# A graph layer whose spilled node terms are written to the output early and completed there by accumulating DMAs

## The reference, cut to what matters

```python
h = jnp.maximum(_layernorm(x, axis=-1), 0.0)          # 100000 nodes x 64
z = jnp.concatenate([h[src], h[dst], edge_attr], -1)   # 25000 edges x 160
m = jax.nn.sigmoid(z @ W_f + b_f) * jax.nn.softplus(z @ W_s + b_s)
message = jax.ops.segment_sum(m, src, num_segments=100000)
mean = jnp.mean(message, axis=0)
var = jnp.mean((message - mean) ** 2, axis=0)
normed = (message - mean) * jax.lax.rsqrt(var + 1e-5) * gamma + beta
return x + h + normed
```

## Time and profile before

| | before |
|---|---|
| median of 3 runs | 1061.29 us (1059.76 to 1061.81) |
| the profiled execution: its own time | 1060.81 us |
| its span, first to last instruction | 1059.1 us |
| first stage, about | 0 to 846 us |
| scan | 846 to 924 us |
| variance, scale and shift | 924 to 927 us |
| final stage | 927 to 1059 us |
| busy share of the span: PE, DVE, ACT, POOL | 60%, 69%, 51%, 69% |
| bytes moved by DMA | 176.07 MB |

### The profile page before, as it was taken

How to read it: one execution, slowest core, us unless ns; L and a number is a source line. 1 busy time by engine, 2 the same in 40 slices (tenths; PEclk the granted TensorE clock), 3 DMA queues, 4 the chain that set the end, 5 groups by cost and what they waited for, 6 DMA issues and landing times.

```text
span 1059.1 us, 11028 instructions
## 1 busy us (share of the span) xinstructions
PE 631.5 (60%) x2458; PEld 453.8 (43%) x2458; DVE 733.2 (69%) x1547; ACT 540.0 (51%) x1181; POOL 729.9 (69%) x652
## 2 busy tenths in 40 slices
PE   0474665666566666656766666676556689944232
PEld 0252444454444444444544454554445578810000
DVE  3884675757575686766777666776666569699788
ACT  1263654545454665545565464655646564434322
POOL 6777878787877877777878777787878752430700
PEclk9855565555555565556555555655656689955555
DMA  8997534343434334333443333433433399799999
GB/s 320 397 394 275 126 96 106 96 106 94 106 94 106 74 86 87 61 81 61 79 87 61 80 71 70 87 63 79 85 56 59 35 380 420 247 302 426 413 404 377
DMA packets 88183, 176.07 MB, mean 166 GB/s; under 512 B 42575, under 2 KB 49299, under 8 KB 79699
## 3 DMA queue, kind: packets, MB, share of 16 engines
q1 hardware_dynamic: 35851, 115.32, 30.9%
q0 software_dynamic: 42880, 20.09, 15.4%
q10 hardware_dynamic: 9416, 40.29, 9.3%
HBM read 107.12 MB, written 68.53 MB: 166 GB/s over the span
## 4 chain that ended last, share of the span: by engine, by line
POOL 48%; DMA 24%; issue 17%; DVE 6%; PE 3%; ACT 1%; SPq 1%; POOLq 0%; ACTq 0%; DVEq 0%
POOL msgs_dram L607 24%; POOL m_buf L594 24%; DMA m_buf<-msgs_dram 8%; DMA msgs_dram<-y_kept 8%; DMA msgs_dram<-sums,target 6%; PE ps_all L1544 2%; DVE m_buf L1795 2%; DMA out_dram<-m_buf 2%; DVE m_buf L1801 1%; DVE sums L1717 1%; PE ps_all L1539 0%; SPq L499 0%; POOL m_buf L617 0%; DVE target L794 0%; DVE m_buf L763 0%
## 5 line engine op out<-in xcount | busy, mean ns | idle before, releaser
L594 POOL DMA_INDIRECT m_buf<-in_x_dram,m_buf x384 | 366.9, 955 | 118.7 <-issue 109.4
L607 POOL DMA_INDIRECT msgs_dram<-sums,target x184 | 289.7, 1574 | 56.2 <-issue 55.8
L1171 PE MATMUL ps_all<-sums,m_last 128*128 128x64 f32 x920 | 188.5, 394 | 124.8 <-ACT m_last L1033 107.1
L1171 PEld LDWEIGHTS ps_all<-sums,m_last 128*128 128x128 f32 x920 | 181.0, 303 | 136.2 <-issue 112.5
L719 DVE TENSOR_REDUCE m_last<-late 128x24 f32<-128x1536 f32 (+1 forms) x49 | 85.3, 1742 | 87.8 <-ACT late L984 87.8
L1131 PE MATMUL ps_all<-ident,m_buf 128*128 128x128 f32 x192 | 53.0, 431 | 128.6 <-DVE m_buf L809 128.6
L1145 PEld LDWEIGHTS ps_all<-m_buf 128*128 128x128 f32 x392 | 91.9, 322 | 49.0 <-issue 49.0
L794 DVE TENSOR_TENSOR target<-moved,m_last 128x4 int32<-128x4 f32 x49 | 9.6, 196 | 146.1 <-POOLq L605 145.8
L1033 ACT ACTIVATE m_last<-m_last,one_col 128x512 f32<-128x512 f32 x196 | 107.6, 550 | 1.6
L1131 PEld LDWEIGHTS ps_all<-ident,m_buf 128*128 128x128 f32 x192 | 34.9, 217 | 160.4 <-DVE m_buf L809 138.5
L1143 PE MATMUL ps_all<-m_buf 128*128 128x512 f32 x98 | 98.8, 1111 | 0.0
(11 more groups left out here) (171 smaller groups left out, 1078.1 us busy)
## 6 DMA issues: line engine op xcount, KB each, us to landing
m_buf<-msgs_dram SPq DMA_DIRECT2D x38, 1024.0 KB, 11.9
m_buf<-in_x_dram SPq DMA_DIRECT2D x48, 512.0 KB, 5.0
msgs_dram<-y_kept SPq DMA_DIRECT2D x14, 1536.0 KB, 11.0
out_dram<-m_buf ACTq DMA_DIRECT2D x20, 1024.0 KB, 11.2
m_buf<-src_rows_dram SPq DMA_DIRECT2D x47, 256.0 KB, 4.1
y_spill_dram<-y_kept ACTq DMA_DIRECT2D x19, 512.0 KB
y_kept<-y_spill_dram SPq DMA_DIRECT2D x8, 1024.0 KB, 12.1
m_buf<-in_x_dram,m_buf POOLq DMA_INDIRECT x392, 2.5
```

The costliest lines, as they stand in the source:

```text
L594: pool.indirect_dma_start(xg[:, n % G_SLOTS, 2 * j + c, :], None, x, bass.IndirectOffsetOnAxis(ap=ids[:, c, n * TILES + j:n * TILES + j + ...
L607: pool.indirect_dma_start(msgs, bass.IndirectOffsetOnAxis(ap=target[:, n % UNROLL, j:j + 1], axis=0), comb[:, n % COMB_SLOTS, j, :], None, ...
L1171: pe.matmul(ps_c[:, j, :], same_of(b, j, j + 1)[:, 0, :], msg_of(g)[:, b, :], start=(b == 0 and not begun), stop=(b == j), skip_group_chec ...
```

## The change

- ACT writes the spilled y straight to its rows of the output (`at.out_rows`), and nothing loads it again.
- The list `order` is now: the 8 held blocks, block 24, the spilled blocks 0 to 9 (i = 9 to 18), then blocks 10 to 15 (i = 19 to 24). For a spilled block DVE computes message * scale and adds shift from SBUF; POOL then issues an accumulating DMA of the block onto the output (`merge`). The loads that take over these buffers wait for its landing (`merged`). The three groups of four patches stand on POOL between merges.
- For the 15 other blocks ("kept parts") PE adds the whole shift as an fp32 product of one row. No part has its mean taken or beta added ahead, and `split_shift` is gone.
- Blocks 13 to 23 have 20 rows squared, where blocks 13 to 21 had 16 and blocks 22 and 23 had 12; the three banks are used from block 15 on, not 19.

```diff
-SQ_THEN_ROWS = 16
+SQ_THEN_ROWS = 20
-SQ_CHANGE = 19
+SQ_CHANGE = 15
...
-            act.dma_start(y_spill[:, bass.ds(row, BULK), :],
+            act.dma_start(at.out_rows[:, bass.ds(row, BULK), :],
                           y_kept[:, bass.ds(row, BULK), :]).then_inc(spilled, 16)
...
-        if b >= NB - 1 - FEW_SQUARED:
-            return [(0, n, FEW_ROWS)]
...
-    order = held + [NB - 1] + list(range(SPILLED_BLOCKS, NB - 1 - M_BUFS)) + list(range(SPILLED_BLOCKS))
+    order = held + [NB - 1] + list(range(SPILLED_BLOCKS)) + list(range(SPILLED_BLOCKS, NB - 1 - M_BUFS))
...
+    def wait_stored(eng, i):
+
+        eng.wait_ge(merged[buf_of(i)] if merges(i) else stored[buf_of(i)], 16 * stores_of(i))
...
         for k, i in enumerate(in_ring[M_BUFS:]):
             r0, n = BLOCKS[order[i]]
-            sp.wait_ge(stored[buf_of(i)], 16 * stores_of(in_ring[k]))
+            wait_stored(sp, in_ring[k])
             sp.dma_start(m_buf[:, buf_of(i), 0:n, :], m_rows[:, r0:r0 + n, :]).then_inc(m_loaded[buf_of(i)], 16)
-            for b in y_loads[Y_AHEAD + k:Y_AHEAD + k + 1]:
-                load_y(b)
...
             for c in range(0, n, BANK_ROWS):
                 w = min(BANK_ROWS, n - c)
-                ins = pe.matmul(ps_y(k)[:, c:c + w, :], weights, row.unsqueeze(1).to_broadcast([row.shape[0], w, F]),
+                ins = pe.matmul(ps_y(k)[:, c:c + w, :], ones[0:1, :],
+                                shift[0:1, :].unsqueeze(1).to_broadcast([1, w, F]),
                                 start=False, stop=True, skip_group_check=True)
...
-        for k in range(Y_FIRST, BETA_PARTS):
-            add_row(k, ones[0:1, :], bet[0:1, :])
-        pe.wait_ge(split_done, 1)
-        for k in range(BETA_PARTS, len(y_parts)):
-            add_row(k, ones_b[:, :], shift_row[0:SPLIT, :])
+        pe.wait_ge(shift_ready, 1)
+        for k in kept_parts:
+            add_row(k)
...
+        def merge(i):
+
+            k = next(k for k, (of, _, _) in enumerate(y_parts) if of == i)
+            r0, n = BLOCKS[order[i]]
+            pool.wait_ge(added, k + 1)
+            pool.dma_start(out_rows[:, r0:r0 + n, :], m_out(i, 0, n), accum_op=ALU.add).then_inc(merged[buf_of(i)], 16)
...
+            if merges(i):
+                dve.tensor_tensor(m, m, shift[:, :].unsqueeze(1).to_broadcast([P, n, F]), ALU.add).then_inc(added, 1)
+            else:
+                dve.wait_ge(y_summed, kept_parts.index(k) + 1)
+                dve.tensor_tensor(m, m, ps_y(k), ALU.add).then_inc(added, 1)
```

More of the change, by code:

```diff
@@ L1281, in stage_two @@
     stored = [sem(f"stored{i}") for i in range(M_BUFS + 1)]
+    merged = [sem(f"merged{i}") for i in range(M_BUFS)]
     rest_stored = sem("rest_stored")
@@ L1366, in wait_m, with merges @@
             eng.wait_ge(m_loaded[b], 16 * loads)
+    def merges(i):
+        return order[i] < SPILLED_BLOCKS
     def stores_of(i):
-        return len([k for k, _, _ in y_parts if k <= i and buf_of(k) == buf_of(i)])
+        return len([k for k, _, _ in y_parts if k <= i and buf_of(k) == buf_of(i) and merges(k) == merges(i)])
+    def wait_stored(eng, i):
+        eng.wait_ge(merged[buf_of(i)] if merges(i) else stored[buf_of(i)], 16 * stores_of(i))
     def y_of(b):
[L1374 to L1387, removed]
+        r0 = BLOCKS[b][0] - SPILL * BULK
+        return y_kept[:, r0:r0 + BLOCKS[b][1], :]
     def part_rows(i):
@@ L1393, in stage_two @@
                for r in range(0, BLOCKS[b][1], part_rows(i))]
[L1395 to L1398, removed]
+    kept_parts = [k for k, (i, _, _) in enumerate(y_parts) if not merges(i)]
+    bank_of, filled = {}, 0
+    for k in kept_parts:
+        bank_of[k] = filled % PSUM_BANKS
+        filled += (y_parts[k][2] + BANK_ROWS - 1) // BANK_ROWS
+        assert bank_of[k] * BANK_ROWS + y_parts[k][2] <= PSUM_BANKS * BANK_ROWS
     def banks(k):
@@ L1406, in held_by @@
     def held_by(k):
-        return max([j + 1 for j in range(k) if banks(j) & banks(k)], default=0)
+        return max([j + 1 for j in kept_parts if j < k and banks(j) & banks(k)], default=0)
     first_held = BLOCKS[held[0]][0]
@@ L1507, in scalar @@
         act.activation(var[:, :], lnv[:, :], ACT.Exp, scale=-0.5).then_inc(rstd_ready, 1)
-        copied = Y_FIRST + 1
+        waiting = kept_parts[Y_FIRST + 1:]
         for k in range(-1, len(y_parts)):
-            if k >= 0:
+            if k >= 0 and not merges(y_parts[k][0]):
                 i, r, n = y_parts[k]
@@ L1524, in scalar @@
         for k in range(M_BUFS + 1):
-            last = max(i for i in range(NB) if buf_of(i) == k)
+            last = max(i for i in range(NB) if buf_of(i) == k and not merges(i))
             act.wait_ge(stored[k], 16 * stores_of(last))
@@ L1799, in vector @@
             dve.wait_ge(scaled, k + 1)
-            dve.wait_ge(y_summed, k + 1)
-            dve.tensor_tensor(m, m, ps_y(k), ALU.add).then_inc(added, 1)
+            if merges(i):
[3 more added lines that the diff above has]
+                dve.tensor_tensor(m, m, ps_y(k), ALU.add).then_inc(added, 1)
             if i == len(held) - 1 and y_parts[k + 1][0] > i:
```

96 lines of the change are left out of this document (26 added, 70 removed).

## The result

The changed kernel takes 1091.47 us (median of 4 runs, 1091.09 to 1094.87), the kernel before 1061.15 (1059.76 to 1061.81, 4 runs). The ratio is 1.0295, with a 95% interval of 1.0271 to 1.0318: the change costs 30 us. The prediction said 1083 in a range of 1066 to 1109, slower with a chance of 88%.

A forecast was written before the change was run, and what follows sets the result against it. Bounds: PE in the scan, DMAs in the final stage. First merge at 990.0 after PE's slow row, then 82.7 us of DMAs, 7 of patches, about 1 of landing: span 1081; plus 1.7 and 0.5 gives 1083 us, range 1066 to 1109.

The forecast's parts named there:

- the scan's gain: Scan: shift ready about 4.8 us earlier, with bounds of nothing and 8 us.
- Shift is ready near 922.4: End of scan: DVE, no longer PE, sets the end; shift ready near 922.4, against 927.2 counted before.
- a scan that still ends at 923: Scan: listed sign that the forecast is wrong; if right, the diagonal starts near 919, after DVE.
- the bound that the prediction named: Scan: the gain of about 4.8 us becomes nothing if ACT and DVE stop each other over their three banks.
- PE's row at 1.2 GHz sets the pace for nine blocks: Final stage, first 9 blocks: PE's fp32 row takes 1.71 us a bank, 60.9 us in all, 922.4 to 983.3.
- DVE through the merged blocks, 43.1 us: Final stage, spilled blocks: DVE at its own pace, 9 x 4.52 + 2.4 = 43.1 us, from 985.5 to 1028.6.
- A merge costs 2 units: Final-stage DMAs: accumulating a block takes 2 units, a unit being 2.545 us of all engines for a full block.
- From the first added block to the end, 91 us: Final stage from 990.0 to 1081: 32.5 units or 82.7 us, 7 us of patches, about 1 us of last landing.
- Rival 3: Final stage: PE's clock rises to 2.4 GHz, first 9 blocks end 21 us earlier; chance 12%, of which 8 faster.
- 49.4 units: Final stage before the change: 15.5 units of second loads, 9.5 of spilled y, 24.4 of stores; 126 us.
- 17 + 32.5 = 49.5 units: Final-stage DMAs after the change: 17 units (43 us) in the first nine blocks, 32.5 (82.7 us) from the first merge.

The follow-up runs named there:

- e11: Changed kernel with the three groups of patches put behind merges 9, 11 and 13 instead of from the 14th on: 1090.72 us, ratio 1.0279.
- e3: Changed kernel with PE adding shift as an fp32 product of 128 equal rows (shift/128 each) instead of one row: 1075.37 us, ratio 1.0140.
- e10: Changed kernel with the 128-row product and 20 rows squared only in even blocks from 14 on, merges kept: 1070.93 us, ratio 1.0094.
- e9: Kernel before (y reloaded) without means, beta rows and split, with the 128-row product and 20 rows squared only in even blocks from 14: 1060.31 us, ratio 0.9998.
- e1_plain: Changed kernel whose ten merges store and do not add, so outputs of spilled rows lack y: 1074.88 us, ratio 1.0137.

## Why the prediction was right, and what it mis-sized

The direction and the mechanisms of the final stage held; the scan's gain did not come, and with it and the tail go the 8.4 us between the span forecast (1081) and measured (1089.4). By its own steps:

- **Shift is ready near 922.4: wrong, it was 928.5**, later than before (927.7 in the trace, 927.2 as the prediction counts it) and not earlier. This is the step that failed, and the prediction's own sign for it, a scan that still ends at 923, came: the diagonal started at 923.90. It did start behind DVE and not behind PE, as said. 6.1 us fall into three pieces. DVE's last stretch began 2.7 us later (first L1691 behind L941 at 899.48, where it had begun at 896.78), for the third chunk of block 13. The prediction counted that chunk's 0.42 us, and not that it stands ahead of what starts the stretch; with 16 rows in that block (e4) the stretch began at 896.82. The stretch then took 24.5 us and not 22.1, 2.4 us more: its operations took what was counted (21.1 us), but DVE was idle for 3.5 us ahead of the chunks, 2.5 of them ahead of those of 8 rows as the group below has it, where it had been for 1.3:

```profile
L1691 DVE TENSOR_TENSOR sums<-sums,ps_all 128x512 f32<-128x512 f32 x21 | 14.4, 686 | 2.5 <-ACT ps_all L1450 0.6
```

  From 905 to 923 us ACT waited 4.2 us for DVE's sums, so that the two holding each other up at the banks, the bound that the prediction named (a gain of nothing), is likely; the trace names ACT for only 0.6 us of DVE's own gaps, and no run parts them. The last 1.1 us are PE's small products between diagonal and shift, which ran at the lower clock after PE had been idle from 918.9 to 924.3 us: 4.57 us where 3.5 were read. A window over them in the changed kernel:

```profile
924.00:927.00 3.00, 2.37 (x10) 2.21 (x10) 0.78 (x3) 0.00 (x0) 2.39 (x3) 0.50 0.41 21
```

  The kernel before had 1.00 there, as its PE had come from the block's products with a pause of 0.5 us.
- **PE's row at 1.2 GHz sets the pace for nine blocks: right.** 61.18 us against 60.9 (the "277 rows" are 285, and the 35.6 banks go by 285); DVE's waits for it of 2.3 us a block; a DMA share of 0.72 to 0.75.
- **DVE through the merged blocks, 43.1 us: right**, from 991.8 to 1035.0.
- **A merge costs 2 units: right**, 2.02.
- **From the first added block to the end, 91 us: 93.0.** The tail is the piece that was mis-sized: the last stores wait for patches queued behind the merges, and the engines run half empty for 9.4 us after 1080, where 1 us was allowed. e11 took the tail away and gained nothing by it. DVE waited for loads, as said, but only from i = 22 on and not from 19, for 9.0 us.
- **Rival 3, a clock that rises: did not happen**, from 924 to the end the granted clock is 0.50, 1.2 GHz. Its price of 21 us was somewhat high: in e3, with 2.4 GHz from 936 us on, the first merge comes 17.5 us earlier and the time falls by 16.

What the prediction didn't see is the reason behind the sum. It counted 49.4 units before and found a longer time for 17 + 32.5 = 49.5 units after, and put it all on PE. e10 shows a second cause, when PE is gone: 10 us stay, with equal DMA work (151.1 and 151.7 us). Reload and store cost what a merge costs, but the reloads are issued from 912 us on, 15 us ahead of shift, and no merge can be. This was measured as idle time of the engines (18.2 us, against 7.4 in the kernel before and 5.5 in e9).

## What to carry to other kernels

Before bytes are traded for an accumulating DMA, count it as two: the saved reload is paid back in the engines. Then ask which of the two can be issued early. When a stage is bound by DMA, work that can run ahead of it is worth more than as much work that can't, and a comparison of idle DMA time over a fixed window shows it in a few rows.

When a chunk is added to an engine's in-order stream, look at what stands behind it and who waits for that, not at its length: an addition of 0.42 us cost 4.3 us here.

## What the runs showed of the hardware

**The granted clock was 0.50 under a product of one row and 1.00 under the same product of 128 rows.** The group of PE's row from 940 to 980 us, in the changed kernel and in e3_rows128 (1*128 and 128*128 are the weights, 1x512 and 128x512 the moving operand: one row and 128):

```profile
L1511 PE MATMUL ps_all<-sums,ones 1*128 1x512 f32 x48 | 41.2, 1056 | 0.0
```

```profile
L1513 PE MATMUL ps_all<-shift_part,ones 128*128 128x512 f32 x70 | 32.4, 606 | 7.7 <-ACT ps_all L1443 7.6
```

One row, without a pause for 61 us: clock 0.50 throughout. 128 rows, the same columns and the same type, with 7.7 us of pauses: clock 1.00. It rose between 934 and 936 us (0.66 in that window, 1.00 in the next), in the midst of these products. As nothing else differs in the product, its rows, or the data in them, made the difference, and no run tells these two apart. With three bf16 rows (e2) it stays at 0.50 as well, but there PE was busy for only 9.2 of 20 us. The Trainium skill (TensorE: Matmul & The Clock Gate, Part 1) says that the default is throttled and that sustained matmul activity releases it. The trace agrees for 128 rows, and disagrees for one row, which ran for 61 us without a pause at 0.50. A product of 128 equal rows thus did the work of one row at twice the clock, 606 ns a record against 1056, and without `split_shift`.

**An accumulating DMA from SBUF to HBM** of rows of 8 KB took 2.08 times the engine time of the same store (5.15 and 2.48 us for 1 MB), and POOL's issue of one took 0.84 to 0.94 us, where that of a plain one (e1_plain) took 0.53 to 0.63.
